# Selective-scan recurrences on one core: the skip term of block 0 moved between two rows of B, and the copy of a group's row of B moved behind the group's first decay

## The chip, the cores and the metric

The kernel runs on one core of a Trainium2 chip. The metric is device microseconds of one execution. The profile is one profiled execution of the same program.

## The reference

An image of 8 x 16 x 16 tokens with 64 channels passes a deformable convolution, a bidirectional Mamba layer and a graph-attention-gated mixture of four experts, each with a residual. The change is in the Mamba layer alone, whose core is, for each direction:

```
dt = softplus(dbc[..., :16] @ dt_proj_w.T + dt_proj_b)
Bm = dbc[..., 16:32];  Cm = dbc[..., 32:48];  A = -exp(A_log)
dA  = exp(dt[..., None] * A)                     # decay
dBu = dt[..., None] * Bm[:, :, None, :] * xs[..., None]
h_t = dA_t * h_{t-1} + dBu_t                     # along the 256 tokens of an image
y = einsum('blds,bls->bld', hs, Cm) + xs * D     # sum over the 16 states, and the skip term
y = y * silu(z)
```

There are 128 inner channels (the partitions), 16 states, 2 directions and 2048 tokens.

## The kernel before

The recurrences are cut into 4 blocks: direction 0 or 1 (`d`), first or second half of the batch (`hf`), so a tile of a block is 128 x 1024 fp32. A block takes its 16 states one after the other, in groups of four (`GROUP`). Five engines work on it in a pipeline, each with its own program; semaphores alone order them.

For state n of a block, with e = n mod 2 the buffer:

- TensorE spreads the state's row of B over all partitions into PSUM banks 6e and 6e+1 (`rows`, L775) and its row of C into banks 2 and 3 (`rows_c`, L783), each with 2 bf16 matmuls of 512 columns. Banks 4 and 5 collect y: the skip term opens them (L815, `diag_d` times `xs`, fp32), and `add_state` (L790) adds a state's C * h by an identity matmul, fp32.
- ScalarE computes the decay `da[e]` by Exp (L1050) and copies the row of C from PSUM to `cs[e]` (L1057), since GpSimd does not read PSUM here.
- VectorE multiplies B by dt * x in PSUM (L1425) and runs the scan into `hh[e]` (L1435).
- GpSimd multiplies `hh[e]` by `cs[e]` into `gg[e]` (L520), which `add_state` takes.

The last state of a group has another way for its row of B: TensorE puts the row into banks 2 and 3 (`rows_c` with slot 0 of the group), ScalarE copies it to `bx` (`b_copy`, L1043), GpSimd multiplies it by dt * x (`own_b`, L512) and ScalarE puts the product back into PSUM (L1054). Banks 2 and 3 so pass five rows a group in turn: the row of B, then four rows of C. `c_psum` counts the rows written and `c_ready` the rows copied out, and TensorE writes the next row only when the last one is copied out. The decays, the states and the gated products are double-buffered: the decay of state n waits for scan n-2 (`scan_ready`), the C copy of n and scan n for the C product of n-2 (`g_ready`), the C product of n for the add of n-2 (`g_used`).

TensorE's order at the start of a block (`first_rows`, then L808 on) is: row of B of state 3 (to be copied), row of B of state 0, row of C 0, row of B 1, row of C 1, row of B 2, row of C 2, row of C 3, the skip, adds 0 and 1. Between blocks `first_rows` of the next block stands ahead of the last two adds of the block. In the loop it is: row of B of the group's last state, then for each r of 4 the row of B (not for r = 3), the row of C, and the add of the state two before.

ScalarE's order is: `b_copy(0)` ahead of the first loop; `states(grp)`: for each r the decay, at r = 3 the put, and the C copy; then `b_copy` of the next group. Ahead of the loops of each direction ScalarE waits for dt of that direction and for `da_zero`, with which VectorE says that the first column of each image (no decay) is zero in both `da`; for direction 1 VectorE writes these zeros when all scans of block 1 are done (`no_decay`, L1417). Copies need no function table of their own; Exp and Silu (used just before the recurrences) have different ones.

`gated` (L1441) multiplies y by silu(z) when all adds of a block are done.

Of the kernel before, what the change touches and what calls it, by code (L numbers as in the profile page):

```python
# [14 lines left out]
DI, DS, DTR, TAPS = 128, 16, 16, 4  # L15
SEQP = SEQ + 2 * (TAPS - 1)
HALF = T // 2
# [28 lines left out]
GROUP = 4  # L46
# [30 lines left out]
def program(nc, a, out):  # L77
    with ExitStack() as ctx:
        def sb(name, shape, dt=F32):
            return ctx.enter_context(nc.sbuf_tensor(name, shape, dt))  # L80
# [5 lines left out]
        ps = ctx.enter_context(nc.psum_tensor("ps", [P, 8, 512], F32))  # L86

        def banks(lo, n, parts=P):
            return ps[0:parts, lo:lo + n, :].rearrange("p b n -> p (b n)")
# [43 lines left out]
        diag_d = [sb(f"diag_d{d}", [P, P]) for d in range(2)]  # L133
# [99 lines left out]
        xs, zs, dtv, uu = ([ar(T)] for _ in range(4))  # L233
# [339 lines left out]
        def _(pe):  # L573
# [183 lines left out]
            for c in range(CAP):  # L757
                m = pe.matmul(ps[:, 6, 0:2 * W], own1[:, c, :], pay[:, c, :, :].rearrange("p h w -> p (h w)"),
                              start=(c == 0), stop=(c == CAP - 1))
# [11 lines left out]
            def rows(d, hf, i0, n, e):  # L771

                pe.wait_ge(s["scan_ready"], n + 1)
                for q in range(2):
                    m = pe.matmul(ps[:, 6 * e + q, :], sel[:, i0].to_broadcast([96, P]),  # L775
                                  bc3[d][0:96, hf * HALF + 512 * q:hf * HALF + 512 * q + 512], start=True, stop=True)
                m.then_inc(s["b_psum"], 1)

            def rows_c(d, hf, i0, slot):

                pe.wait_ge(s["c_ready"], slot + 1)
                for q in range(2):
                    m = pe.matmul(ps[:, 2 + q, :], sel[:, i0].to_broadcast([96, P]),  # L783
                                  bc3[d][0:96, hf * HALF + 512 * q:hf * HALF + 512 * q + 512], start=True, stop=True)
                m.then_inc(s["c_psum"], 1)

            def add_state(n, e):
                pe.wait_ge(s["g_ready"], n + 3)
                for q in range(2):
                    m = pe.matmul(ps[:, 4 + q, :], ident[:], gg[e][:, 512 * q:512 * q + 512], start=False, stop=True, skip_group_check=True)  # L790
                m.then_inc(s["g_used"], 1)

            def first_rows(blk):
                d, hf = blk // 2, blk % 2
                pe.wait_ge(s["bc_ready"], d + 1)
                rows_c(d, hf, slice(GROUP - 1, GROUP), 4 * blk * SLOTS)
                for e in range(2):
                    rows(d, hf, slice(e, e + 1), 16 * blk + e, e)
                    rows_c(d, hf, slice(DS + e, DS + e + 1), 4 * blk * SLOTS + 1 + e)

            pe.wait_ge(s["z_ready"], 4)
            pe.wait_ge(s["rest_ready"], 4)
            pe.wait_ge(s["diag_ready"], 2)
            first_rows(0)
            for blk in range(4):
                d, hf = blk // 2, blk % 2

                rows(d, hf, slice(2, 3), 16 * blk + 2, 0)  # L808
                rows_c(d, hf, slice(DS + 2, DS + 3), 4 * blk * SLOTS + 3)
                rows_c(d, hf, slice(DS + 3, DS + 4), 4 * blk * SLOTS + 4)  # L810
                if blk:
                    pe.wait_ge(s["yg_ready"], blk)
                for q in range(2):
                    c0 = hf * HALF + 512 * q
                    pe.matmul(ps[:, 4 + q, :], diag_d[d][:], xs[d][:, c0:c0 + 512], start=True, stop=True)  # L815
                for e in range(2):
                    add_state(16 * blk + e, e)
                with pe.Fori(0, DS // GROUP - 1) as it:
                    n, slot = it * GROUP + 16 * blk, it * SLOTS + (4 * blk + 1) * SLOTS
                    rows_c(d, hf, bass.ds(it * GROUP + 7, 1), slot)  # L820
                    for r in range(GROUP):
                        if r < GROUP - 1:
                            rows(d, hf, bass.ds(it * GROUP + (4 + r), 1), n + (4 + r), r % 2)
                        rows_c(d, hf, bass.ds(it * GROUP + (DS + 4 + r), 1), slot + (1 + r))
                        add_state(n + (2 + r), r % 2)
                if blk < 3:
                    first_rows(blk + 1)
                    for e in range(2):
                        add_state(16 * blk + DS - 2 + e, e)
# [57 lines left out]
            for n in range(2 * EXP):  # L887
                h, e = n // EXP, n % EXP
# [12 lines left out]
        def _(act):  # L901
# [138 lines left out]
            def b_copy(grp):  # L1040

                act.wait_ge(s["c_psum"], grp * SLOTS + 1)
                f(bx, banks(2, 2), ACT.Copy).then_inc(s["c_ready"], 1)  # L1043

            def states(grp, src, lo, d, column):

                for r in range(GROUP):
                    n, e = grp * GROUP + r, r % 2
                    act.wait_ge(s["scan_ready"], n + 1)
                    f(da[e].rearrange("p (b s) -> p b s", s=SEQ)[:, :, lo:lo + SEQ - 1], src, ACT.Exp,  # L1050
                      scale=neg_a[d][:, column(r)]).then_inc(s["da_ready"], 1)
                    if r == GROUP - 1:
                        act.wait_ge(s["bx_ready"], grp + 1)
                        f(banks(6, 2), bx, ACT.Copy).then_inc(s["bx_put"], 1)  # L1054
                    act.wait_ge(s["c_psum"], grp * SLOTS + (r + 2))
                    act.wait_ge(s["g_ready"], n + 1)
                    f(cs[e], banks(2, 2), ACT.Copy).then_inc(s["c_ready"], 1)  # L1057

            act.wait_ge(s["nega_ready"], 4)
            for d in range(2):  # L1060
                act.wait_ge(s["dt_ready"], d + 1)
                act.wait_ge(s["da_zero"], 2 + d)
                lo = 1 - d
                for hf in range(2):
                    blk, c0 = 2 * d + hf, hf * HALF
                    src = dtv[d][:, c0:c0 + HALF].rearrange("p (b s) -> p b s", s=SEQ)[:, :, lo:lo + SEQ - 1]
                    if blk == 0:
                        b_copy(0)
                    with act.Fori(0, DS // GROUP if blk < 3 else DS // GROUP - 1) as it:
                        states(it + 4 * blk, src, lo, d, lambda r: bass.ds(it * GROUP + r, 1))  # L1070
                        b_copy(it + (4 * blk + 1))
                    if blk == 3:
                        states(15, src, lo, d, lambda r: slice(DS - GROUP + r, DS - GROUP + r + 1))
            f(pause[:, 3:4], ident[:, 0:1], ACT.Sqrt)
            act.wait_ge(s["ln_var"], 9)
            f(lns[:, 4, :], lns[:, 3, :], ACT.Sqrt).then_inc(s["ln_std"], 1)
# [651 lines left out]
```

## Time and profile before

| | |
|---|---|
| median of 3 runs | 688.21 us (681.62, 688.21, 688.95) |
| profiled execution, time | 686.99 us |
| its span, first to last instruction | 685.2 us |
| mean granted TensorE clock | 0.846 |
| busy: TensorE, VectorE, ScalarE, GpSimd | 528.6, 590.9, 320.2, 324.0 us |

The recurrences take about the stretch from 317 to 545 us of the span. A granted clock of 1.00 is 2.4 GHz and 0.50 is 1.2 GHz. Times in rows are microseconds from the start of the span. In a timeline a row is `start, duration, engine, line, operation, output<-inputs, shapes, count`, and in brackets the idle time of the engine before it with what ended it.

### The profile page before, as it was taken

How to read it: one execution, taken by the hardware profiler on the slowest of the kernel's cores; microseconds unless marked ns; L12 is line 12 of the kernel's file. 1: busy time of each engine (PE TensorE's matmuls, PEld its weight loads, DVE VectorE, ACT ScalarE, POOL GpSimd, SP SyncE). 2: the span in 40 equal slices, each digit the busy share in tenths (PEclk: the TensorE clock that was granted, in tenths of full speed). 3: DMA queues.
4: the chain of work that ended last, by engine and by line, in shares of the span. 5: the costliest groups of instructions: out<-in, count | busy, mean ns of one | idle time of the engine just before them, and what ended most of it. 6: DMA issues, size and time to landing. Idle time of an engine off the chain costs nothing.

```text
span 685.2 us, 11129 instructions
## 1 busy us (share of the span) xinstructions
PE 528.6 (77%) x4061; PEld 342.3 (50%) x4061; DVE 590.9 (86%) x1233; ACT 320.2 (47%) x380; POOL 324.0 (47%) x198
## 2 busy tenths in 40 slices
PE   2669999999999994987787788788888887973200
PEld 2148898898898992532323333233333474642200
DVE  4999799999799959998688989989989748379997
ACT  1431324333113125788577677777767603242210
POOL 5134042022020100235677789879978806777303
PEclk9855999999999996995799999999999985555555
DMA  7400000000000001000000000000000001111000
GB/s 210 101 14 1 2 3 2 3 10 2 2 10 2 2 9 44 0 0 1 0 0 0 0 1 0 0 0 0 1 0 0 0 1 16 9 9 8 4 0 31
DMA packets 17983, 8.56 MB, mean 12 GB/s; under 512 B 14832, under 2 KB 17168, under 8 KB 17680
## 3 DMA queue, kind: packets, MB, share of 16 engines
q1 hardware_dynamic: 16144, 7.35, 4.0%
q0 software_dynamic: 1792, 0.58, 1.5%
q8 instruction: 30, 0.49, 0.3%
q14 instruction: 17, 0.14, 0.1%
HBM read 6.67 MB, written 1.25 MB: 12 GB/s over the span
## 4 chain that ended last, share of the span: by engine, by line
PE 47%; DVE 27%; issue 10%; POOL 7%; ACT 6%; DMA 1%; ACTq 0%; POOLq 0%; DVEq 0%; SPq 0%
PE ps L637 10%; PE ps L629 9%; POOL arena L520 6%; PE ps L656 6%; PE ps L790 5%; DVE arena L1435 3%; PE ps L614 3%; DVE arena L1622 2%; DVE g L1624 2%; DVE ps L1425 2%; PE ps L880 2%; ACT arena L1050 2%; PE ps L893 1%; PE ps L783 1%; ACT arena L1057 1%
## 5 line engine op out<-in xcount | busy, mean ns | idle before, releaser
L520 POOL TENSOR_TENSOR arena<-arena 128x1024 f32<-128x1024 f32 x64 | 150.2, 2356 | 37.4 <-DVE arena L1435 13.4
L1435 DVE TENSOR_TENSOR_SCAN arena<-arena,ps 128x1024 f32<-128x1024 f32 x64 | 144.6, 2280 | 16.0 <-ACT arena L1050 11.8
L790 PE MATMUL ps<-arena,ident 128*128 128x512 f32 x256 | 122.0, 603 | 16.0 <-POOL arena L520 15.6
L485 POOL TENSOR_TENSOR arena<-arena 128x1280 f32<-128x1280 f32 x16 | 39.7, 2505 | 155.9 <-DVE arena L1285 140.1
L790 PEld LDWEIGHTS ps<-arena,ident 128*128 128x128 f32 x256 | 46.8, 191 | 68.2 <-issue 36.3
L954 ACT ACTIVATE arena<-ps 128x768 f32<-128x768 f32 x48 | 37.7, 809 | 89.5 <-PE ps L656 89.5
L1057 ACT ACTIVATE arena<-ps 128x1024 f32<-128x1024 f32 x64 | 65.1, 1018 | 29.1 <-POOL arena L520 23.5
L558 POOL DMA_INDIRECT arena<-node_rows,src_idx x56 | 56.0, 1000 | 37.1 <-DMA node_rows<-hrow 20.3
L1050 ACT ACTIVATE arena<-arena,neg_a 128x1020 f32<-128x1020 f32 x64 | 72.9, 1139 | 0.6 <-DVE arena L1417 0.4
L783 PE MATMUL ps<-arena,sel 96*128 96x512 bf16 x160 | 50.1, 395 | 26.0 <-ACT arena L1057 12.5
L629 PE MATMUL ps<-arena 128*128 128x64 f32 x576 | 70.0, 283 | 0.0
L637 PE MATMUL ps<-arena 128*32 128x64 bf16 x2048 | 69.8, 319 | 0.0
L629 PEld LDWEIGHTS ps<-arena 128*128 128x128 f32 x576 | 69.3, 201 | 0.1
L637 PEld LDWEIGHTS ps<-arena 128*32 128x32 bf16 x2048 | 67.7, 145 | 3.1 <-issue 3.1
L1270 DVE TENSOR_SCALAR arena<-lo_b 128x296 bf16<-128x296 bf16 (+1 forms) x448 | 65.8, 228 | 0.0
L1425 DVE TENSOR_TENSOR ps<-arena,ps 128x1024 f32<-128x1024 f32 x48 | 58.1, 1210 | 7.3 <-PE ps L775 7.3
L656 PE MATMUL ps<-ident,arena 128*128 128x128 f32 x288 | 46.2, 315 | 5.4 <-POOL arena L485 4.7
L656 PEld LDWEIGHTS ps<-ident,arena 128*128 128x128 f32 x288 | 37.5, 161 | 17.9 <-issue 11.3
L783 PEld LDWEIGHTS ps<-arena,sel 96*128 (+1 forms) x160 | 13.4, 99 | 63.8 <-issue 33.7
L1268 DVE TENSOR_SCALAR arena<-hi_b 128x296 bf16<-128x296 bf16 (+1 forms) x224 | 35.4, 237 | 10.6 <-PE ps L637 10.6
L937 ACT ACTIVATE arena<-ps 128x288 f32<-128x288 f32 x32 | 13.1, 410 | 55.4 <-PE ps L629 27.6
L880 PEld LDWEIGHTS ps<-w,arena 128*128 128x128 f32 x128 | 28.2, 331 | 19.5 <-ACT arena L1086 11.5
(333 smaller groups left out, 809.7 us busy)
## 6 DMA issues: line engine op xcount, KB each, us to landing
arena<-dram_edges SPq DMA_DIRECT2D x2, 1024.0 KB, 8.6
arena<-dram_x SPq DMA_DIRECT2D x2, 512.0 KB, 4.8
arena<-node_rows,src_idx POOLq DMA_INDIRECT x56, 2.7
x_tok<-dram_x SPq DMA_DIRECT2D x1, 512.0 KB, 10.9
res_scratch<-x_tok SPq DMA_DIRECT2D x4, 128.0 KB, 2.0
arena<-res_scratch SPq DMA_DIRECT2D x1, 512.0 KB, 3.3
w<-dram_w SPq DMA_DIRECT2D x3, 128.0 KB, 2.7
arena<-dram_f_conv_w SPq DMA_DIRECT2D x1, 256.0 KB, 11.0
```

The source lines that it names most:

```text
L520: g.tensor_tensor(gg[r % 2], hh[r % 2], cs[r % 2], ALU.mult).then_inc(s["g_ready"], 1)
L558: g.indirect_dma_start(out=nb[:, w, :], out_offset=None, in_=tab_d, in_offset=bass.IndirectOffsetOnAxis(ap=src_idx[:, w:w + 1], axis=0)).t ...
L629: m = pe.matmul(o, s_t[i % 2][:, 2 * t + tau, :], xk[b % 2][:, tau, C * t:C * t + C], start=(t == 0 and tau == 0), stop=(t == K2 - 1 and t ...
L637: m = pe.matmul(ps[32 * q:32 * q + 32, 4, 0:LO], one_hi[:, :, e + q], one_lo[:, :, e + q], start=(ch == 0 and e == 0), stop=(ch == len(CHU ...
L656: m = pe.transpose(ps[:, 2 * (n % 2) + v // 4, (v % 4) * P:(v % 4) * P + P], s_rows[i % 2][:, t // 2, (t % 2) * P:(t % 2) * P + P], ident[:])
L783: m = pe.matmul(ps[:, 2 + q, :], sel[:, i0].to_broadcast([96, P]), bc3[d][0:96, hf * HALF + 512 * q:hf * HALF + 512 * q + 512], start=True ...
L790: m = pe.matmul(ps[:, 4 + q, :], ident[:], gg[e][:, 512 * q:512 * q + 512], start=False, stop=True, skip_group_check=True)
L1050: f(da[e].rearrange("p (b s) -> p b s", s=SEQ)[:, :, lo:lo + SEQ - 1], src, ACT.Exp, scale=neg_a[d][:, column(r)]).then_inc(s["da_ready"], 1)
L1057: f(cs[e], banks(2, 2), ACT.Copy).then_inc(s["c_ready"], 1)
L1270: m = ts(one_lo[:, x - HI, 0:en], lo_b[:, e0:e0 + en], float(x - HI), None, ALU.is_equal)
L1425: tt(b, uu[d][:, c0:c0 + HALF], b, ALU.mult).then_inc(s["b_made"], 1)
L1435: v.tensor_tensor_scan(o, x0, x1, 0.0, ALU.mult, ALU.add).then_inc(s["scan_ready"], 1)
```

## The change

Three edits: the skip term becomes a function; for block 0 it is issued in `first_rows` between row of B 0 and row of C 0, for the other blocks it stays where it was. `b_copy` of a group moves into `states`, behind the group's first decay and ahead of its first C copy. With that the B copy ahead of the first loop and those at the end of the loops go, and block 3's last group needs no code of its own. The number of copies, decays and matmuls is the same.

```diff
+            def skip_path(blk):
+                d, c0 = blk // 2, (blk % 2) * HALF
+                for q in range(2):
+                    pe.matmul(ps[:, 4 + q, :], diag_d[d][:], xs[d][:, c0 + 512 * q:c0 + 512 * q + 512], start=True, stop=True)
+
             def first_rows(blk):
                 d, hf = blk // 2, blk % 2
                 pe.wait_ge(s["bc_ready"], d + 1)
                 rows_c(d, hf, slice(GROUP - 1, GROUP), 4 * blk * SLOTS)
                 for e in range(2):
                     rows(d, hf, slice(e, e + 1), 16 * blk + e, e)
+                    if e == 0 and blk == 0:
+                        skip_path(0)
                     rows_c(d, hf, slice(DS + e, DS + e + 1), 4 * blk * SLOTS + 1 + e)
@@ L810
                 rows_c(d, hf, slice(DS + 3, DS + 4), 4 * blk * SLOTS + 4)
                 if blk:
                     pe.wait_ge(s["yg_ready"], blk)
-                for q in range(2):
-                    c0 = hf * HALF + 512 * q
-                    pe.matmul(ps[:, 4 + q, :], diag_d[d][:], xs[d][:, c0:c0 + 512], start=True, stop=True)
+                    skip_path(blk)
                 for e in range(2):
                     add_state(16 * blk + e, e)
@@ L1049, states
                     f(da[e].rearrange("p (b s) -> p b s", s=SEQ)[:, :, lo:lo + SEQ - 1], src, ACT.Exp,
                       scale=neg_a[d][:, column(r)]).then_inc(s["da_ready"], 1)
+                    if r == 0:
+                        b_copy(grp)
                     if r == GROUP - 1:
@@ L1064
-                    if blk == 0:
-                        b_copy(0)
-                    with act.Fori(0, DS // GROUP if blk < 3 else DS // GROUP - 1) as it:
+                    with act.Fori(0, DS // GROUP) as it:
                         states(it + 4 * blk, src, lo, d, lambda r: bass.ds(it * GROUP + r, 1))
-                        b_copy(it + (4 * blk + 1))
-                    if blk == 3:
-                        states(15, src, lo, d, lambda r: slice(DS - GROUP + r, DS - GROUP + r + 1))
```

## Rows read from the trace of the kernel before

**Rows 1.** the page, busy time of each engine, its share of the span and its instructions

```profile
PE 528.6 (77%) x4061; PEld 342.3 (50%) x4061; DVE 590.9 (86%) x1233; ACT 320.2 (47%) x380; POOL 324.0 (47%) x198
```

**Rows 2.** list of waits: engine, line, waited for; us in total, times, longest

```profile
DVE arena L1435 <- ACT arena L1050: 11.8, 16, 2.2
```

**Rows 3.** timeline of TensorE, start of block 0

```profile
317.87 1.06 PE L775 MATMUL ps<-arena,sel 96*128 96x512 bf16 x2
319.96 1.04 PE L783 MATMUL ps<-arena,sel 96*128 96x512 bf16 x2 [1.04 <-ACT arena L1043]
...
329.00 1.03 PE L783 MATMUL ps<-arena,sel 96*128 96x512 bf16 x2 [2.37 <-ACT arena L1057]
329.82 3.62 PE L815 MATMUL ps<-arena,diag_d 128*128 128x512 f32 x4
333.24 3.80 PE L790 MATMUL ps<-arena,ident 128*128 128x512 f32 x8
```

**Rows 4.** windows: PE, PEld, DVE, ACT, POOL busy (instructions), PEclk, DMA

```profile
310.00:313.00 3.00, 3.00 (x4) 1.08 (x4) 2.96 (x2) 2.97 (x3) 0.38 (x1) 0.50 0.00 0
333.50:334.00 0.50, 0.50 (x2) 0.21 (x2) 0.44 (x1) 0.00 (x0) 0.00 (x0) 0.87 0.00 0
```

**Rows 5.** timelines of GpSimd and VectorE, block 0 and first scan of block 1

```profile
335.47 4.65 POOL L520 TENSOR_TENSOR arena<-arena 128x1024 f32<-128x1024 f32 x2 [4.65 <-PE ps L790]
...
337.94 1.23 DVE L1425 TENSOR_TENSOR ps<-arena,ps 128x1024 f32<-128x1024 f32 x1 [4.00 <-PE ps L775]
341.02 2.29 DVE L1435 TENSOR_TENSOR_SCAN arena<-arena,ps 128x1024 f32<-128x1024 f32 x1 [1.86 <-ACT arena L1050]
...
355.46 2.29 DVE L1435 TENSOR_TENSOR_SCAN arena<-arena,ps 128x1024 f32<-128x1024 f32 x1 [1.77 <-ACT arena L1050]
...
382.76 2.29 DVE L1435 TENSOR_TENSOR_SCAN arena<-arena,ps 128x1024 f32<-128x1024 f32 x1 [0.19 <-ACT arena L1050]
```

**Rows 6.** timelines of ScalarE and TensorE, block 0, start of group 2

```profile
351.95 1.02 ACT L1043 ACTIVATE arena<-ps 128x1024 f32<-128x1024 f32 x1 [1.39 <-PE ps L783]
352.99 1.28 ACT L1050 ACT_TABLE_LOAD   x1
354.28 1.15 ACT L1050 ACTIVATE arena<-arena,neg_a 128x1020 f32<-128x1020 f32 x1
...
353.11 0.60 PE L783 MATMUL ps<-arena,sel 96*128 96x512 bf16 x2 [0.77 <-ACT arena L1043]
...
355.27 0.60 PE L775 MATMUL ps<-arena,sel 96*128 96x512 bf16 x2
```

**Rows 7.** timelines of VectorE, GpSimd and ScalarE, block 0, second state of group 2

```profile
357.67 1.21 DVE L1425 TENSOR_TENSOR ps<-arena,ps 128x1024 f32<-128x1024 f32 x1
359.01 2.29 DVE L1435 TENSOR_TENSOR_SCAN arena<-arena,ps 128x1024 f32<-128x1024 f32 x1
...
361.53 2.35 POOL L520 TENSOR_TENSOR arena<-arena 128x1024 f32<-128x1024 f32 x1 [1.17 <-ACT arena L1057]
...
363.97 1.02 ACT L1057 ACTIVATE arena<-ps 128x1024 f32<-128x1024 f32 x1 [0.49 <-POOL arena L520]
```

**Rows 8.** timelines of ScalarE and VectorE, block 1, starts of groups

```profile
409.07 1.02 ACT L1043 ACTIVATE arena<-ps 128x1024 f32<-128x1024 f32 x1 [1.39 <-PE ps L783]
...
398.14 2.29 DVE L1435 TENSOR_TENSOR_SCAN arena<-arena,ps 128x1024 f32<-128x1024 f32 x1 [0.43 <-ACT arena L1050]
...
411.16 2.29 DVE L1435 TENSOR_TENSOR_SCAN arena<-arena,ps 128x1024 f32<-128x1024 f32 x1 [0.35 <-ACT arena L1050]
```

**Rows 9.** timelines of ScalarE, TensorE and GpSimd, passage to block 2

```profile
434.95 1.02 ACT L1043 ACTIVATE arena<-ps 128x1024 f32<-128x1024 f32 x1 [0.89 <-PE ps L783]
436.41 1.15 ACT L1050 ACTIVATE arena<-arena,neg_a 128x1020 f32<-128x1020 f32 x1 [0.44 <-DVE arena L1417]
...
438.52 0.60 PE L783 MATMUL ps<-arena,sel 96*128 96x512 bf16 x2 [1.46 <-ACT arena L1057]
...
440.93 2.35 POOL L520 TENSOR_TENSOR arena<-arena 128x1024 f32<-128x1024 f32 x1 [0.31 <-PE ps L790]
```

## The prediction

> **What bounds the kernel now.** The busy times come first: VectorE 86% and TensorE 77% of the span, ScalarE and GpSimd 47% each [rows 1]. That is an average over stages; the change touches only the recurrences (about 317 to 545 us), so the rest was read there. The list of waits says what VectorE lacks in that stretch: before its 64 scans it sat idle 11.8 us, always until ScalarE's decay (L1050) [rows 2]. Then the timelines of the engines, side by side, give the order of one group of four states. Names used below: *B copy* (L1043), *decay* (L1050), *put* (L1054), *C copy* (L1057) on ScalarE; *row* of B or C (L775, L783), *skip* (L815), *add* (L790, one state, four matmuls) on TensorE; *product* (L1425) and *scan* (L1435) on VectorE; the products with B (L512) and C (L520) on GpSimd.
>
> VectorE alone needs, for a group, 4 scans and 3 products: a scan takes 2.20 us until the next instruction starts (355.46 to 357.67), a product 1.34 until its scan starts [rows 5, 7], so 4 x 2.20 + 3 x 1.34 = 12.8 us. GpSimd needs 5 x 2.35 = 11.8 [rows 7]. Block 0 runs at 355.46 - 341.02 = 14.44 us a group [rows 5]. The excess is a wait of 1.77 before the group's first scan [rows 5], and rows 6 show its cause: the last C copy of the group ends 1.39 before 351.95, ScalarE idles those 1.39 for the row of B, does the B copy (1.02), loads a function table (1.28) and only then the decay (1.15), which ends as the scan starts. In block 1 no table is loaded and the same wait is 0.35 [rows 8]. Apart from that, the first block has one long hole: TensorE does the skip (3.4) and two adds (3.8) from 329.8 to 337.0 [rows 3], at a granted clock of 0.50 that rises to 1.00 just after 333.5 (0.87 is the mean of that half microsecond) [rows 4]; GpSimd idles 4.65 for the first add, VectorE 4.00 for the next row of B and then 1.86 for the decay [rows 5].
>
> **Part 1: the skip term of block 0, from behind the rows to between them.** The same four matmuls (3.41 us at the low clock: 333.24 - 329.82 [rows 3]) now follow the two rows of B, the second of which starts at 317.87 and takes 0.85 or so: 318.8 [rows 3]. TensorE's next instruction, the first row of C, waits for the B copy. That copy, which ends just before 319.96 today, comes behind the table load and the first decay, 1.3 + 1.05 later: near 322.3. The skip ends at 318.8 + 3.4 = 322.2: hidden. Without that cover (B copy early) it would cost up to 322.2 - 319.96 = 2.2 us to the first row of C. What is late next: nothing before 329.0. The last row of C, with 2.37 idle before it [rows 3], waits for a C copy behind GpSimd's first products, and GpSimd starts those behind work that does not move. So the adds start at 329.82 and not at 333.24. Their time depends on the clock. If it rises at 333.57 as now, the first add ends at 333.2 (low clock, 3.4), the second at 335.1; row of B and row for the product by 336.1; product; scan at 337.5. The decay is ready long before: ScalarE has nothing else to do from the group's last C copy on, and load and decay take 2.4. That is 3.5 us before 341.02 [rows 5]. Bounds: with the high clock throughout, the adds end at 333.3, and the second scan of the group, which then waits for the row behind the B copy, gains 4.9; with the low clock throughout, the adds end at 336.7, the scan starts near 339.2 and gains 1.8. I take 3.5, since the pattern of work from 329.0 on is as dense as before.
>
> **Part 2: the decay ahead of the B copy, block 0.** The decay and its table load leave the path (B row, B copy, load, decay, scan). From the end of the last C copy, load and decay take 2.4 us and fit before the product is done, so group 2's scan is set by VectorE: 12.8 after 337.5, at 350.3; 14.44 - 12.8 = **1.6** gained. But the B copy now stands behind load and decay, and behind it the row of C, an add, the row for the second product, all in TensorE's order. From the end of the last C copy: load 1.30, decay to the next start 1.05 (1.15 less the 0.1 by which a copy and a decay back to back overlap), B copy 1.02, gap to the row of C 0.14, row of C and add 355.27 - 353.11 = 2.16, row for the product 0.6 [rows 6] = 6.3; product to scan 1.34, scan to GpSimd's product 361.53 - 359.01 = 2.52, that to the C copy 363.97 - 361.53 = 2.44, C copy 1.02 [rows 7] = 7.3. The loop takes 13.65 us: a new bound, 0.8 above VectorE's 12.85. So group 3 (counted from 0) gains 14.44 - 13.65 = **0.8**, and the passage to block 1, where VectorE's idle is only 0.19 today (no table is loaded) [rows 5], loses **0.8**. Block 0 in all: 3.5 + 1.6 + 0.8 - 0.8 = **5.1 us** gained at the first scan of block 1.
>
> The rows give the load 1.29 from its start to the decay's, with no gap before it [rows 6]; the sum uses that. The Trainium skill ("ScalarE: Activation LUTs", What ACT_TABLE_LOAD costs) gives 1283 ns for the load and another 1380 ns of drain for a switch; by that price three loads on the new loop would cost 4.1 more, and the whole change would gain 1.3, which is rival (d). The trace has the 1.28 and not the drain.
>
> **Part 3: the same in blocks 1 to 3.** The decay takes 1.05 of ScalarE's 1.39 of idleness before the B copy [rows 8], so the B copy stays where it is and GpSimd and TensorE see nothing. VectorE's idle before the scan is 0.43 at a block's second group and 0.35 at the next two [rows 8], of which 1.34 - 1.21 = 0.13 stays, as between any product and its scan [rows 7]: 0.3 + 0.2 + 0.2 = **0.7** a block, 2.1 in three. Bounds: 0, if ScalarE's decay is held up by the loop's turn, and 0.43 + 0.35 + 0.35 = 1.1 a block.
>
> **Part 4: the passage from block 1 to block 2.** Here the moved copy meets a wait. The decay of the backward direction waits for the zeros that VectorE writes (L1417) behind the last scan of block 1; ScalarE waits for that before it enters the loop. Today the B copy is done before (434.95 to 435.97), now it is queued behind the wait and the decay: decay 436.41, B copy 437.46 to 438.5 [rows 9]. Behind it on TensorE stand a row of C, a row of B, the next row of C (438.52 today, behind the first C copy; now B copy 438.5, gap and row 0.74, C copy 1.02, gap 0.06: 440.3), and two adds. GpSimd idles 0.31 for the first add already [rows 9], so the chain from there to the skip and the adds of block 2 has no slack. Cost 440.3 - 438.52 = **1.8 us**. Bounds: 0, were the chain to have slack that I do not see, and 2.5, the whole shift of the B copy.
>
> **Sum.** -5.1 - 2.1 + 1.8 = **-5.4 us**. The profiled run took 686.99 (span 685.2, 1.8 around it), so the new kernel would take 681.6; the median of three runs is 688.21, 1.2 higher, which gives 682.8. I say **682**. The tail behind 545 us depends on the recurrences' end alone and moves as a whole.
>
> **Rivals.** *(a) The clock rises earlier.* With the skip between the rows TensorE works almost without a gap from 317 to 326, where today it idles 1.04 and more [rows 3]. If the clock rises then and holds, part 1 gives 4.9 and not 3.5; and a run of before in which it rises late (up to 3.4 later, a low-clock add) loses 1.7 more to it: -6.8 to -8.5, 679 to 681. Against it: from 310 to 313 TensorE was busy throughout and the clock stayed at 0.50 [rows 4], and behind the rows comes an idle of over 2 us [rows 3]. The Trainium skill ("TensorE: Matmul & The Clock Gate", Part 1) says the throttled state is the default and activity releases it, which speaks for this rival; the trace agrees as far as its one rise in this stretch, behind the skip, goes.
> *(b) The loads leave block 0's loop* or are hidden otherwise: then block 0 runs at 12.8, and the loss of 0.8 at its end goes as does 0.8 in group 3: -7, 680. Against it: the loop body is entered with the table of Silu, and the load stands at the first Exp of the body today [rows 6].
> *(c) Slower: the B copy slips in every group.* Its cover is ScalarE's idle of 1.39 against a decay of 1.05 [rows 8]. If the decay can't start when the C copy ends, the B copy slips by up to 1.05; it decides once the cover left is under 1.05. Of the row for the second product only 0.4 is slack: it ends at 409.07 + 1.02 + 0.14 + 2.16 + 0.6 = 413.0, and VectorE takes it at 411.16 + 2.20 = 413.4 [rows 6 to 8]. Eleven groups of blocks 1 to 3 at 0.65 are +7.2 in the place of -2.1: -5.1 + 7.2 + 1.8 = +3.9, 692. For it speaks only the thin margin of 0.34.
> *(d) The load costs more in its new place than its row shows*: a second 1.3 in three groups of block 0, +3.9, leaves -1.5: 686. Against it: the row.
>
> **How the numbers follow.** Forecast 0.54, (a) 0.22, (b) 0.06, (c) 0.06, (d) 0.12. The range takes in (a), (b) and half of (d): 677.5 to 686.5; runs of this kernel spread over 681.6 to 689.0, so about 1% (6.9 us) is what can be told from no change. The forecast of -5.4 lies inside; with its own spread of 2 us a quarter of it lies beyond: 0.13 + 0.18 of (a) + 0.03 of (b) gives 0.34 faster, 0.62 same, 0.04 slower.
>
> **What would show it.** Skip matmuls at about 318.8, none between rows and adds; GpSimd's idle of 4.65 down to about 2.5 and VectorE's 4.00 to about 2.2; first scans of block 0's groups 1 to 3 near 337.5, 350.3, 364.0, block 1's near 377.6; product to scan 1.34 everywhere; table loads still four, each ahead of the B copy; in block 2 the B copy at decay + 1.05 and the skip 1.8 later than today against the scan that opens the block. Wrong would be: a different clock history between 317 and 337, a B copy late in the plain groups, or no loss at block 2.

## The result, and the profile after

| | before | after |
|---|---|---|
| median of 21 runs each, alternating | 683.13 us (679.07 to 689.35) | 677.21 us (671.19 to 685.84) |
| mean of the same runs | 684.1 | 678.9 |
| profiled execution, span | 685.2 us | 674.5 us |
| mean granted TensorE clock of it | 0.846 | 0.865 |

The ratio is 0.988, 95% interval 0.985 to 0.991. It leaves out 9 runs of after as disturbed, so it shows more than the means do: they differ by 5.1 us, 0.75%, with a standard error of 1.25. Both kernels' 21 runs lie in two heaps: before has 11 at 679.1 to 683.1 and 10 at 685.5 to 689.4, after 11 at 671.2 to 677.2 and 10 at 680.5 to 685.8, and each median is the uppermost run of its lower heap. With all later runs of after (30) its heaps hold 14 and 16, with nothing between, and the mean is 679.4 +- 0.9; some 90 runs of before, later ones among them that fill its gap, have a mean of 683.8 +- 0.3. The better figure for the change is this 4.4 us.

The profiles differ by 10.7 us, and that is no measure of the change. I cut each span at four landmarks on VectorE: the last write of zeros ahead of the recurrences (L1417 before, L1420 after; where the head ends), the first scan of blocks 1, 2 and 3, and the start of the last two scans (where the tail begins). Beside the two profiles stand four more of each kernel, from the experiments:

| us | span | head | block 0 | block 1 | block 2 | block 3 | blocks, sum | tail |
|---|---|---|---|---|---|---|---|---|
| before | 685.2 | 318.65 | 64.11 | 54.83 | 54.20 | 48.50 | 221.6 | 144.9 |
| before, e7 | 677.3 | 309.34 | 63.89 | 54.81 | 55.89 | 48.50 | 223.1 | 144.9 |
| before, e11 | 684.8 | 317.94 | 64.41 | 54.82 | 54.20 | 48.52 | 222.0 | 144.9 |
| before, e13 | 677.5 | 309.48 | 63.87 | 54.81 | 55.90 | 48.52 | 223.1 | 144.9 |
| before, e15 | 679.5 | 312.89 | 64.19 | 54.83 | 54.18 | 48.51 | 221.7 | 144.9 |
| after | 674.5 | 313.07 | 60.83 | 54.18 | 56.73 | 47.86 | 219.6 | 141.8 |
| after, e6 | 669.9 | 309.65 | 58.84 | 54.16 | 57.63 | 47.86 | 218.5 | 141.8 |
| after, e12 | 673.3 | 313.12 | 60.84 | 54.15 | 56.74 | 47.85 | 219.6 | 140.6 |
| after, e14 | 683.7 | 318.40 | 58.99 | 54.16 | 57.71 | 49.42 | 220.3 | 145.0 |
| after, e16 | 680.2 | 314.77 | 59.01 | 54.15 | 57.74 | 49.43 | 220.3 | 145.1 |

Of the 10.7 us, 5.6 lie in the head, where not one instruction is changed, 2.0 in the recurrences and 3.1 in the tail. The means of five and five say: head 313.7 and 313.8, so nothing; recurrences 222.3 and 219.7, **-2.6**; tail 144.9 and 142.9, **-2.0**. That is -4.5, near the -4.4 of the times. The agreement is no test: the heads scatter by 3 to 4 us from profile to profile, so that two means of five could have differed by 2 or 3 us by chance. The recurrences scatter by 0.7 only, and their -2.6 is clear of that.

The head first. A window of before, then the same of after (columns: us, busy time with instructions of PE, PEld, DVE, ACT, POOL, granted clock, DMA share, GB/s), and below each the same 36 matmuls from the timeline of TensorE:

```profile
45.00:62.00 17.00, 17.00 (x67) 13.98 (x66) 17.00 (x98) 5.28 (x8) 1.74 (x2) 0.50 0.00 0
...
54.42 7.78 PE L629 MATMUL ps<-arena 128*128 128x64 f32 x36
```

```profile
45.00:62.00 17.00, 12.42 (x152) 10.41 (x155) 17.00 (x98) 5.15 (x9) 1.73 (x2) 0.80 0.01 2
...
49.82 4.13 PE L629 MATMUL ps<-arena 128*128 128x64 f32 x36
```

The same 36 matmuls took 7.78 us at a granted clock of 0.50 and 4.13 in after, where the clock had risen. (The counts 67 and 152 exaggerate the difference: some 80 of the 152 are short matmuls of the next line, which after had already reached.) The slow head is no mark of before: e14, a profile of after, has one of 318.40. Whoever compares two profiles of this kernel has to take that out first.

**The recurrences of after.** The page's busy times (to [rows 1]) and the list of waits (to [rows 2]):

```profile
PE 508.2 (75%) x4061; PEld 326.8 (48%) x4061; DVE 591.1 (88%) x1233; ACT 321.3 (48%) x380; POOL 323.8 (48%) x198
...
L1438 DVE TENSOR_TENSOR_SCAN arena<-arena,ps 128x1024 f32<-128x1024 f32 x64 | 144.7, 2281 | 8.2 <-ACT arena L1056 2.4
```

```profile
DVE ps L1428 <- PE ps L775: 10.1, 6, 3.0
...
DVE arena L1438 <- ACT arena L1056: 2.4, 4, 1.5
```

The wait that the change aims at is down from 11.8 us in 16 places to 2.4 in 4. VectorE's wait for a row of B from TensorE has grown, from 7.3 us in 5 places to 10.1 in 6. Before had:

```profile
DVE ps L1425 <- PE ps L775: 7.3, 5, 4.0
```

Where those of after come from, the timeline of TensorE shows (to [rows 3]):

```profile
312.15 1.06 PE L775 MATMUL ps<-arena,sel 96*128 96x512 bf16 x2
313.00 2.66 PE L797 MATMUL ps<-arena,diag_d 128*128 128x512 f32 x4
316.88 0.61 PE L783 MATMUL ps<-arena,sel 96*128 96x512 bf16 x2 [1.22 <-ACT arena L1049]
...
323.43 1.04 PE L783 MATMUL ps<-arena,sel 96*128 96x512 bf16 x2 [2.27 <-ACT arena L1065]
324.26 5.56 PE L790 MATMUL ps<-arena,ident 128*128 128x512 f32 x8
...
345.14 0.93 PE L783 MATMUL ps<-arena,sel 96*128 96x512 bf16 x2 [1.72 <-ACT arena L1049]
345.86 3.29 PE L790 MATMUL ps<-arena,ident 128*128 128x512 f32 x4
```

The skip (L797) stands between the rows and is hidden: TensorE still waits 1.22 behind it. The clock rose during it (2.66 for what takes 3.62 at the low clock; the rows behind it take 0.60), and was low again at 323.43, behind the idle of 2.27, where a row that takes 0.60 takes 1.04. So the two adds took 5.56 and not the 3.80 of [rows 3]. GpSimd and VectorE (to [rows 5]):

```profile
328.03 4.66 POOL L520 TENSOR_TENSOR arena<-arena 128x1024 f32<-128x1024 f32 x2 [3.45 <-PE ps L790]
...
330.73 1.23 DVE L1428 TENSOR_TENSOR ps<-arena,ps 128x1024 f32<-128x1024 f32 x1 [2.98 <-PE ps L775]
332.09 2.29 DVE L1438 TENSOR_TENSOR_SCAN arena<-arena,ps 128x1024 f32<-128x1024 f32 x1
...
344.89 2.29 DVE L1438 TENSOR_TENSOR_SCAN arena<-arena,ps 128x1024 f32<-128x1024 f32 x1
349.62 1.23 DVE L1428 TENSOR_TENSOR ps<-arena,ps 128x1024 f32<-128x1024 f32 x1 [2.44 <-PE ps L775]
...
360.25 2.29 DVE L1438 TENSOR_TENSOR_SCAN arena<-arena,ps 128x1024 f32<-128x1024 f32 x1
...
373.90 2.29 DVE L1438 TENSOR_TENSOR_SCAN arena<-arena,ps 128x1024 f32<-128x1024 f32 x1
```

The idle times of 4.65 and 4.00 are now 3.45 and 2.98, and the 1.86 before the scan is gone. Group 1 to group 2 takes 12.80. Then comes 15.36, since the add at 345.86 fell to the low clock too (3.29; 1.88 is usual). The last group takes 13.65. The adds of block 0 start 11.19 behind the last zeros (324.26 - 313.07), as forecast (329.82 - 318.65 = 11.17). ScalarE at the start of group 1, and in the passage to block 2 (to [rows 6, 9]):

```profile
326.29 1.28 ACT L1056 ACT_TABLE_LOAD   x1
327.58 1.15 ACT L1056 ACTIVATE arena<-arena,neg_a 128x1020 f32<-128x1020 f32 x1
330.30 1.02 ACT L1049 ACTIVATE arena<-ps 128x1024 f32<-128x1024 f32 x1 [1.57 <-PE ps L783]
...
426.90 1.15 ACT L1056 ACTIVATE arena<-arena,neg_a 128x1020 f32<-128x1020 f32 x1 [2.13 <-DVE arena L1420]
427.96 1.00 ACT L1049 ACTIVATE arena<-ps 128x1024 f32<-128x1024 f32 x1
```

The load keeps its 1.28 and the decay follows 1.29 behind its start. At 427.96 the B copy stands behind the wait for zeros and the decay, as forecast. What that does to TensorE:

```profile
425.41 0.59 PE L775 MATMUL ps<-arena,sel 96*128 96x512 bf16 x2
429.01 0.61 PE L783 MATMUL ps<-arena,sel 96*128 96x512 bf16 x2 [3.01 <-ACT arena L1049]
...
430.74 1.04 PE L783 MATMUL ps<-arena,sel 96*128 96x512 bf16 x2 [0.69 <-ACT arena L1065]
431.57 4.82 PE L790 MATMUL ps<-arena,ident 128*128 128x512 f32 x8
```

It idles 3.01, and behind that idle the clock falls: the adds take 4.82 where 3.60 is usual.

**The tail.** The same code of the experts' matmuls in before, then in after:

```profile
578.46 3.52 PE L880 MATMUL ps<-w,arena 128*128 128x64 f32 x16
581.90 2.08 PE L893 MATMUL ps<-arena,w 64*128 64x512 f32 x4
```

```profile
570.79 1.90 PE L886 MATMUL ps<-w,arena 128*128 128x64 f32 x16
572.62 1.13 PE L899 MATMUL ps<-arena,w 64*128 64x512 f32 x4
```

In after the clock rose there, in before it stayed at 0.50, and these and the next matmuls of the experts took near twice as long; the tail as a whole differs by 3.1 us.

### The profile page after: what moved, and what is told of

Its sections match the earlier page's. It is cut to its first block, busy times and chain, and to the rows that moved or that the text cites. A ratio compares the mean times of both kernels' runs of the same rounds, so it can differ in the third digit from the quotient of the medians.

```text
span 674.5 us, 11144 instructions
## 1 busy us (share of the span) xinstructions
PE 508.2 (75%) x4061; PEld 326.8 (48%) x4061; DVE 591.1 (88%) x1233; ACT 321.3 (48%) x380; POOL 323.8 (48%) x198
## 3 DMA queue, kind: packets, MB, share of 16 engines
HBM read 6.67 MB, written 1.25 MB: 12 GB/s over the span
## 4 chain that ended last, share of the span: by engine, by line
PE 40%; DVE 26%; POOL 13%; issue 13%; ACT 5%; DMA 2%; DVEq 0%; POOLq 0%; ACTq 0%; SPq 0%
PE ps L637 10%; PE ps L629 8%; POOL arena L558 8%; PE ps L790 5%; PE ps L656 5%; POOL arena L520 5%; DVE arena L1438 4%; DVE ps L1428 4%; PE ps L614 2%; PE ps L711 1%; DVE arena L1273 1%; PE ps L783 1%; ACT arena L1065 1%; PE ps L861 1%; DVE arena L1271 1%
## 5 line engine op out<-in xcount | busy, mean ns | idle before, releaser
L520 POOL TENSOR_TENSOR arena<-arena 128x1024 f32<-128x1024 f32 x64 | 150.1, 2361 | 35.3 <-PE ps L790 16.3
L790 PE MATMUL ps<-arena,ident 128*128 128x512 f32 x256 | 126.3, 621 | 11.8 <-POOL arena L520 11.7
L790 PEld LDWEIGHTS ps<-arena,ident 128*128 128x128 f32 x256 | 48.6, 197 | 65.5 <-issue 38.8
L1428 DVE TENSOR_TENSOR ps<-arena,ps 128x1024 f32<-128x1024 f32 x48 | 58.1, 1211 | 10.2 <-PE ps L775 10.1
L629 PE MATMUL ps<-arena 128*128 128x64 f32 x576 | 66.3, 274 | 0.0
L629 PEld LDWEIGHTS ps<-arena 128*128 128x128 f32 x576 | 65.6, 192 | 0.1
L656 PE MATMUL ps<-ident,arena 128*128 128x128 f32 x288 | 42.2, 297 | 5.4 <-POOL arena L485 4.7
L656 PEld LDWEIGHTS ps<-ident,arena 128*128 128x128 f32 x288 | 34.3, 151 | 17.1 <-issue 11.7
L512 POOL TENSOR_TENSOR arena<-arena 128x1024 f32<-128x1024 f32 x16 | 37.9, 2366 | 0.4 <-ACT arena L1049 0.2
```

Of the source, the lines that this page charges most:

```text
L520: g.tensor_tensor(gg[r % 2], hh[r % 2], cs[r % 2], ALU.mult).then_inc(s["g_ready"], 1)
L629: m = pe.matmul(o, s_t[i % 2][:, 2 * t + tau, :], xk[b % 2][:, tau, C * t:C * t + C], start=(t == 0 and tau == 0), stop=(t == K2 - 1 and t ...
L656: m = pe.transpose(ps[:, 2 * (n % 2) + v // 4, (v % 4) * P:(v % 4) * P + P], s_rows[i % 2][:, t // 2, (t % 2) * P:(t % 2) * P + P], ident[:])
L1428: tt(b, uu[d][:, c0:c0 + HALF], b, ALU.mult).then_inc(s["b_made"], 1)
```

## The experiments

**The two parts alone.** e1: before with the skip between the rows, ScalarE's order as it was. e2: before with the B copy behind the first decay of every group, the skip where it was.

```
e1   first_rows, e == 0 and blk == 0:      + skip_path(0)       (ScalarE as before)
e2   states, behind the decay of r == 0:   + b_copy(grp)        (TensorE as before)
     L1067 to L1073                        - b_copy(0), - b_copy(it + (4 * blk + 1)),
                                           - the last group of block 3 written out
```

> The kernel before with the skip term of block 0 moved and nothing of ScalarE's order changed. In the profiles so far the stretch from VectorE's last zero (L1417 before, L1420 after) to the first scan of block 1 is 64.1 us before and 60.8 us after, block 1 54.8 and 54.2, block 2 54.2 and 56.7, block 3 to its last pair of scans 48.5 and 47.9. Theory A (the skip's move is worth about 3.5 us in block 0 when the clock has the same history, and parts 2 to 4 are as predicted): here TensorE has no cover for the skip at the start (row of C up to 2.2 us later) but GpSimd's first products set the adds anyway, so the stretch to block 1 is 60.5 to 62, blocks 1 to 3 are as before (54.8, 54.2, 48.5). Theory B (the gain of block 0 comes from the decay's new place and the skip's move is eaten by the lower clock that finds the adds): the stretch stays at 63.5 to 64.5. Time: A about 3 us below the kernel before, B within 1 us.

> The kernel before with the B copy behind the group's first decay and the skip term where it was. Theory A: the stretch to the first scan of block 1 is 62 to 63 (the first decay's table load out of the path at group 1 and 2, the new loop of 13.65 us in the last two), block 1 54.2, block 2 54.2 + 1.8 - 0.7 = 55.3 at a steady clock or 56.7 if the longer idle before it lets the clock fall, block 3 47.9. Theory B (all gain of block 0 from the decay): stretch 60.5 to 61. Rival: the loss of block 2 comes with the skip's move and not with the copy's: block 2 54.2 here.

First scans of groups 1, 2, 3 and of block 1, from the last zeros:

| us | group 1 | group 2 | group 3 | block 1 |
|---|---|---|---|---|
| before | 22.37 | 36.81 | 51.26 | 64.11 |
| e1, skip alone | 20.60 | 35.04 | 49.49 | 62.34 |
| e2, copy alone | 20.58 | 33.38 | 47.04 | 60.70 |
| e6, both (after again) | 18.71 | 31.52 | 45.18 | 58.84 |
| gain: e1, e2, e6 | 1.8, 1.8, 3.7 | 1.8, 3.4, 5.3 | 1.8, 4.2, 6.1 | 1.8, 3.4, 5.3 |

The gains add up. Neither theory of e1 gave its 62.34 (60.5 to 62, or 63.5 to 64.5): the skip alone is worth half of what theory A gave it. e2's 60.70 lies where theory B had it, but not for B's reason, since the skip gains too; theory A had put too little (62 to 63) on the copy. The 1.8 of the skip are 3.4 of skip less the 1.6 by which the adds are slower (5.43 against 3.80). The other 1.8 at group 1, which I had put into part 1, is the copy's: load and decay have left VectorE's path there too. In e2 the adds still lie behind the skip, and are fast; ScalarE did the decay long before:

```profile
328.42 3.62 PE L815 MATMUL ps<-arena,diag_d 128*128 128x512 f32 x4
331.83 3.72 PE L790 MATMUL ps<-arena,ident 128*128 128x512 f32 x8
```

```profile
330.45 1.28 ACT L1050 ACT_TABLE_LOAD   x1
331.74 1.15 ACT L1050 ACTIVATE arena<-arena,neg_a 128x1020 f32<-128x1020 f32 x1
336.03 1.02 ACT L1043 ACTIVATE arena<-ps 128x1024 f32<-128x1024 f32 x1 [3.14 <-PE ps L783]
```

Times: e1 685.05 median of 12, ratio 0.999 (0.996 to 1.002), where 3 us below before had been expected; e2 682.22 of 12, 0.995 (0.991 to 0.998). The ratios here and below are to runs of before taken beside each experiment; the means stand in a table below. e2 pays block 2's passage: 56.66, 2.5 over before.

**The queue at block 2.** e3 is after with the B copy of group 8 ahead of the wait for zeros.

```
   act.wait_ge(s["dt_ready"], d + 1)
+  if d:
+      b_copy(8)
   act.wait_ge(s["da_zero"], 2 + d)
```

The group that follows is written out without a B copy, and the loop runs over groups 9 to 11.

> The changed kernel, but the B copy of the first group of block 2 stands ahead of ScalarE's wait for the zeros of the backward direction, as in the kernel before. If the loss of block 2 (56.7 against 54.2) is that copy queued behind the wait and the decay, block 2 falls to 53.5 (54.2 less 0.7), 3.2 below the changed kernel, of which 1.8 is the queue and the rest the clock that fell in the 3.0 us that TensorE idled there. If the loss was only this run's clock, it stays above 55.5. Time: about 2 to 3 us below the changed kernel.

TensorE of e3 in the passage:

```profile
425.53 0.60 PE L783 MATMUL ps<-arena,sel 96*128 96x512 bf16 x2 [0.74 <-ACT arena L1049]
425.97 0.59 PE L775 MATMUL ps<-arena,sel 96*128 96x512 bf16 x2
427.49 1.04 PE L783 MATMUL ps<-arena,sel 96*128 96x512 bf16 x2 [0.92 <-ACT arena L1065]
428.32 4.85 PE L790 MATMUL ps<-arena,ident 128*128 128x512 f32 x8
```

The idle of 3.01 is 0.74, and block 2 takes 54.98 in the place of 56.73 to 57.74. The adds were slow here too, behind an idle of 0.92, so the queue is not the only thing that lets the clock fall at this place; before had slow adds here in two of five profiles (5.29, which is its 55.89). But it makes the fall more frequent: all eight profiles of kernels with the copy queued there (five of after, e2, e4, e5) have slow adds in this passage, against two of seven with the order of before (e1 and e10 among them) and one of three with the mended order (e3, e8, e9). Where they are not slow (e8, e9, with the same order) block 2 takes 53.35. So the queue costs 56.73 - 54.98 = 1.75 with slow adds in both. The 53.5 expected came out in e8 and e9, not in e3. Time: 676.11 median of 6, ratio 0.985 (0.980 to 0.990).

**The loads out of the loop.** e4 is after with one small exponential ahead of the recurrences, which brings the table in once. e10 is the same line in before.

```
+  f(pause[:, 3:4], ident[:, 0:1], ACT.Exp)
   act.wait_ge(s["nega_ready"], 4)
```

> The changed kernel with one Exp of a single column ahead of ScalarE's loops, so that the function table is loaded once and the loop of block 0 has no load in it. Theory A (the load, decay and B copy in a row set the pace of block 0): groups of block 0 go at VectorE's 12.8 us, no table load in the loop, the stretch from the last zero to block 1 is 58 to 59.5 against 60.8. Rival: GpSimd or the clock sets the pace of block 0, and the stretch stays within 0.5 of 60.8. Time: 1 to 3 us below the changed kernel.

> The kernel before with one table load ahead of ScalarE's loops and nothing else. In the order of before each load of block 0 stands on the path to the scan: its groups fall from 14.44 to 13.1 or so (VectorE's 12.8 plus the idle of 0.35 of the later blocks), and the first boundary by 1.3: block 0 64.0 - 1.0 (first scan) - 3 x 1.3 = 59 to 60.3, other blocks as before. If that is so, the table load alone is worth as much in block 0 as the copy's new place (60.7 with the copy moved alone). Time: 3 to 5 us below the kernel before.

ScalarE of e4, end of group 1, no load ahead of the decay, and VectorE's first scans of groups 1 and 2:

```profile
338.52 1.02 ACT L1065 ACTIVATE arena<-ps 128x1024 f32<-128x1024 f32 x1
339.50 1.15 ACT L1056 ACTIVATE arena<-arena,neg_a 128x1020 f32<-128x1020 f32 x1
```

```profile
330.00 2.29 DVE L1439 TENSOR_TENSOR_SCAN arena<-arena,ps 128x1024 f32<-128x1024 f32 x1
...
342.81 2.29 DVE L1439 TENSOR_TENSOR_SCAN arena<-arena,ps 128x1024 f32<-128x1024 f32 x1
```

Every group of block 0 takes 12.80 to 12.81, VectorE's own sum; block 0 ends at 57.14, 1.7 before e6. The loads are what keeps block 0 at 13.66. But this profile of e4 shows no gain over all four blocks: two slow adds (5.30 for 3.60) fell in at the passage to block 1, which takes 55.79 for 54.16, and block 2 takes 57.69, so that the recurrences take 218.5, as in e6. In e10 block 0 takes 59.84: one line gains 4.3 there, more than the copy's move alone (3.4), and leaves the passage to block 2 as it was (54.20). Times: e4 675.16 median of 12, 0.986 (0.982 to 0.990); e10 681.06 of 12, 0.994 (0.990 to 0.998); by the medians alone e10 gains nothing on the 681.21 of before beside it, by the means 3.7 us.

**The idle ahead of the adds filled.** e5 is after with the skip issued a second time, in block 0, just before the last row of C; it writes the same values to the same place, so the output is the same.

```
   rows_c(d, hf, slice(DS + 2, DS + 3), 4 * blk * SLOTS + 3)
+  if blk == 0:
+      skip_path(0)
   rows_c(d, hf, slice(DS + 3, DS + 4), 4 * blk * SLOTS + 4)
```

> The changed kernel with the skip term of block 0 computed a second time, ahead of the block's last row of C, where TensorE idled 2.3 us in the changed kernel; it overwrites the first with the same values, so nothing else changes. It is a filler: 1.7 us of matmuls at the high clock, 3.4 at the low one. Clock theory (the skip raises the clock early, it falls again in the idle that follows, and the eight adds pass at the low clock: 5.3 to 5.6 us against 3.8 before): with the filler the adds take 3.4 to 3.8 us and the first scan of group 1 comes at 17 to 17.7 after the last zero against 19.0 (18.8 without the other things that differ). Rival (the clock's history there is chance or set by what lies before): the adds stay at 5.3 or so, and the filler costs up to 1 us, 19 to 20.

```profile
318.32 3.15 PE L797 MATMUL ps<-arena,diag_d 128*128 128x512 f32 x4
321.31 0.60 PE L783 MATMUL ps<-arena,sel 96*128 96x512 bf16 x2
321.74 3.60 PE L790 MATMUL ps<-arena,ident 128*128 128x512 f32 x8
```

TensorE works without a gap from the filler on, and the adds take 3.60. The filler did not keep the clock up, though. The row of C ahead of it took 1.03, so the clock was low before the filler began (in e6 too: 1.03 ahead of the idle of 1.55), and it rose near the filler's end (3.15; 1.88 would be the high clock, 3.62 the low one). So the filler does what the skip did in before, whose 3.62 at the low clock stood ahead of adds of 3.80: it takes the low clock upon itself. This run can't tell whether the idle or the missing work made the adds slow. The filler also delays them, and group 1 gains 0.8 against e6 (17.88 for 18.71). A slow add then fell in at group 2 (3.37), and block 0 took 59.70. Time: 678.78 median of 12, 0.990 (0.986 to 0.994); its mean of 677.5 against 680.1 of e6 beside it is within the noise, so no gain over after is shown.

**All three, and the two that paid.** e8 is e3 + e4 + e5, e9 is e3 + e4.

> The changed kernel with all three: one table load ahead of the loops, the B copy of block 2's first group ahead of the wait for the zeros, and the second skip term as a filler. Without slow adds: block 0 at 16.5 for the first scan of group 1 and 12.8 a group, 55.5 to 56; blocks 53.9, 53.5 to 55, 47.9; 211 to 213 for the four, against 219.6 of the changed kernel and 221.6 before. Time 7 us below the changed kernel. If the clock falls at the passages between blocks as in the kernel with one table load (5.3 us for eight adds), 214 to 216.

> The changed kernel with one table load ahead of ScalarE's loops and the B copy of block 2's first group ahead of the wait for the zeros, without the filler. From the single runs: block 0 57.1, block 1 53.9, block 2 53.4 without slow adds, block 3 47.9: 212.3 for the four stretches if no adds are slow at the passages, up to 1.8 more for each passage at which they are. Rival: the two mends share one gain (the shorter block 0 only moves the slow adds to later passages, as one table load alone did: 218.5): then 215 or more. Time: 5 to 7 us below the changed kernel at a like head and tail.

VectorE of e9, first scans of groups 1 to 3 and of block 1:

```profile
337.65 2.29 DVE L1446 TENSOR_TENSOR_SCAN arena<-arena,ps 128x1024 f32<-128x1024 f32 x1
...
350.45 2.29 DVE L1446 TENSOR_TENSOR_SCAN arena<-arena,ps 128x1024 f32<-128x1024 f32 x1
...
363.26 2.29 DVE L1446 TENSOR_TENSOR_SCAN arena<-arena,ps 128x1024 f32<-128x1024 f32 x1
...
376.06 2.29 DVE L1446 TENSOR_TENSOR_SCAN arena<-arena,ps 128x1024 f32<-128x1024 f32 x1
```

12.80 a group throughout. e9's recurrences take 212.5 us, e8's 212.9 (block 0 in 56.2, but slow adds of 5.29 at block 3). In e9 the two adds of block 0 are slow (5.55, behind an idle of 3.54); at all later passages they take 3.60. Times: e8 678.25 median of 6, 0.990 (0.984 to 0.995); e9 **672.23** of 6, 668.5 to 674.5, 0.986 (0.983 to 0.990), the fastest kernel here by its median, 5 below after. The 7 us below after that were expected of e8 did not come: 678.25 lies 1 above it.

Means against the runs of before taken beside each (us, with the standard error of the difference):

| e1 | e2 | e3 | e4 | e5 | e6 | e8 | e9 | e10 | e7, before itself |
|---|---|---|---|---|---|---|---|---|---|
| -0.7 +- 0.9 | -2.6 +- 1.1 | -8.8 +- 1.9 | -8.3 +- 1.3 | -6.8 +- 1.5 | -4.2 +- 2.7 | -7.5 +- 1.5 | -10.3 +- 1.2 | -3.7 +- 1.2 | -1.8 +- 1.3 |

**More profiles of the two kernels, unchanged.** e6, e12, e14 and e16 are after; e7, e11, e13 and e15 are before.

> The changed kernel once more, for a second profile and more times. If the stretches follow the program and not chance, the recurrences from the last zero to the last pair of scans take 219 to 220 as in the first profile, with slow adds at the same places (block 0's first, passage to block 2, which took 5.6 and 4.8); if the one slow add in group 2 (3.3 us against 1.9) was chance, block 0 is 59 and not 60.8. The stretches ahead of the recurrences and behind them may differ by up to 6 and 3 us from the first profile, since only the clock's history differs there.

> The kernel before once more, for a second profile. If the first is typical, block 0 takes 64.1, the blocks 54.8, 54.2, 48.5, with no slow adds behind the first. The head (to the last zero, 318.7 in the first profile) lies at 312 to 319: if it comes out below 315, the first profile of before was one of the long heads and its 5.6 us against the changed kernel's head are no effect of the change.

> The kernel before, for a third profile: blocks 63.9 to 64.1, 54.8, 54.2 or 55.9 (with slow adds at the passage to block 2), 48.5. Head between 309 and 319. If the tail is a matter of the program's length, it is 144.9 again as in the two profiles so far; if it is chance, it may come out near 141.7 as in the changed kernel's.

> The changed kernel, for a third profile: block 0 58.9 or 60.8 (with a slow add in group 2), block 1 54.2, block 2 56.7 to 57.6, block 3 47.9; head between 309 and 319; tail 141.8 again if it follows the program, up to 144.9 if it is chance.

> The kernel before once more, unchanged. Theory 1, the shorter tail belongs to the change: the stretch from the last pair of scans to the end is 144.9 us again in this and the two other looks at before, and 140.6 to 141.8 in the three looks at after. Theory 2, chance of the clock: at least one of the six shows the other kernel's tail. Head: 309 to 319, either way by chance.

> The changed kernel once more. Theory 1: tail 140.6 to 141.8, the granted clock rises in the experts' matmuls. Theory 2: in one of the three looks at after the tail is near 145. Block 0 to the first scan of block 1: 58.8 where the adds follow at 5.3, 60.8 where a third slow add falls in, in both theories.

> As for the fourth look at before: tail 144.9 by theory 1; 140.6 to 141.8 in at least one look by theory 2.

> As for the fourth look at after: tail 140.6 to 141.8 by theory 1; near 145 in at least one look by theory 2.

Times: e6 682.53 median of 6, e7 681.32 of 8, the others one run each: e11 686.55, e12 675.01, e13 679.27, e14 685.49, e15 681.25, e16 681.93. Their stretches stand in the table above. By the third profile of each kernel the tail seemed to be the change's (144.9 against 140.6 to 141.8), the theory that e13 to e16 call the first. It fell: e14 and e16 have tails of 145.0 and 145.1. TensorE of e14:

```profile
490.29 1.03 PE L783 MATMUL ps<-arena,sel 96*128 96x512 bf16 x2 [0.69 <-ACT arena L1065]
491.11 4.86 PE L790 MATMUL ps<-arena,ident 128*128 128x512 f32 x8
...
577.02 3.52 PE L886 MATMUL ps<-w,arena 128*128 128x64 f32 x16
```

Both profiles have slow adds at block 3 as well (49.4 for 47.9), as e8 has, whose tail is 145.1 too. Block 3 and tail together make after come in two kinds 4.8 to 6.1 us apart. That is a part of the distance between the heaps, not all of it: the three profiled runs in the lower heap and the two in the upper one are 9.4 us apart in the mean, 5.2 of it by block 3 and tail, and 4.6 by the head. e2 has the long tail without slow adds at block 3, so the one does not simply cause the other. All profiles of kernels without the moved copy (five of before, e1, e10) have the long tail; of the eleven with it (five of after, e2 to e5, e8, e9) seven have the short one, 140.6 to 141.8. Were the tail's kind independent of the copy's place, so clean a split would come about once in a hundred times. So the change probably opens the short tail without making it certain; by what way is not shown, and before might still show it in a longer series.

## Why the prediction was right and wrong

The forecast of -5.4 us was near what the times show: 4.4 to 5.1 by the means, 5.9 by the medians. The time of 682 was not: 677.21 lies 0.3 below the range. The step that failed is **Sum**, at "the median of three runs is 688.21, 1.2 higher, which gives 682.8". The base was 683 to 684 (683.13 by the median of 21 runs, 683.8 by the mean of all), not 688: with these the same change gives 677.7 to 678.4, inside the range. I took one profile and three runs for the kernel's time, while its head alone varies by 9.3 us from profile to profile (309.3 to 318.7), and my profile had the longest head of the five. That the tail "moves as a whole" was the second part of that failure: with the clock it varied between 140.6 and 145.1.

Term by term, against profiles in which nothing else fell in:

| term | forecast | measured |
|---|---|---|
| group 1 of block 0 (part 1) | -3.5 | -3.7 (e6); skip 1.8, copy 1.8 |
| group 2 | -5.1 | -5.3 |
| block 1 (end of part 2) | -5.1 | -5.3; -3.3 where a third add was slow |
| loop of block 0 with the load | 13.65 | 13.66 (e6), 12.80 without load (e4) |
| part 3, a block | -0.7 | -0.65 |
| part 4, queue at block 2 | +1.8 | +1.75 (after against e3) |
| part 4, low clock behind the idle | 0 | +1.2 to +1.8 |
| block 3's passage | 0 | +1.6 in two profiles of five |

**Part 1** was right in its size, and the two adds took what I had summed (5.26 in e6, 5.3 by my sum: low clock for the first, high for the second). The way there was another, which I had named as a sign of being wrong: the clock rose already during the skip and fell again before the adds. That the adds then met the same split is luck. VectorE's idle ahead of group 1 came out at 2.98 (2.49 in e6) and not at 2.2. And part 1 was wrong in what it was made of; half of the gain belongs to the copy. **Part 2** and **part 3** held to 0.2 us; the terms of part 2's loop, 6.3 and 7.3, add up to 13.6, a little under the 13.65 that I wrote and the 13.66 that came. **Part 4** held for the queue and left out what the idle does to the clock. I had asked that question at the start of block 0 and not here. Over five profiles, block 0 gained 4.4 (forecast 5.1, two slow adds in group 2), block 2 lost 2.4 (forecast 1.1), and block 3's gain of 0.65 was eaten up on average: that is how -5.4 became -2.6 in the recurrences. The tail then gave 2.0 back, which no step of mine had. So the total of -5.4 came near the measured one partly by luck.

**Rivals.** (a) The rise came, in the skip of after and e1, but did not hold up to the adds, and they were slow. In after it was lost over the idle of 2.27 that I had set against it; in e6 already one row earlier, behind an idle of 0.91. The Trainium skill ("TensorE: Matmul & The Clock Gate", Part 1) has activity release the throttle. The rise during the skip, and in e5 during the filler (3.15), agree with that. (b) The loads stayed in the loop; e4 shows that taking them out gives what I had put on it. (c) The B copy did not slip in the plain groups: block 1 gained 0.65. (d) No drain: the decay starts 1.29 behind the load's start. The Trainium skill ("ScalarE: Activation LUTs", What ACT_TABLE_LOAD costs) has another 1380 ns there for a switch to a different set. The loop time of 13.66 leaves no room for it. The three loads in the loop's later passes bring in a table that is in already, so the page need not mean them; but the first load of before is such a switch, and it starts 0.02 behind the copy ahead of it, with the decay 1.30 behind its start (319.92 to 321.22).

## What to carry to other kernels

Before a time is forecast, cut the profile at landmarks around the change and ask how much the unchanged stretches vary between executions; here that was 9 us in the head and 4.5 in the tail, around a change of 2.6 in between. When an edit lengthens an idle of TensorE ahead of dense matmuls, price the matmuls behind it at both clocks: here the wait itself cost 1.75 and the fall of the clock as much again. And when a loop on ScalarE is entered with another function table, look for a load in every pass: one small exponential ahead of the loop was worth 4.3 us in the first block in the one profile of e10, more than the move of the copy.

## What was not expected of the hardware

The same instructions at the same place run at either clock level from one execution to the next: in the passage to block 2 of before the two adds took 5.29 in two profiles and kept to their usual 3.60 in three, behind idles of 1.44 to 1.46 in all five. In after, slow adds followed idles of 2.3, 1.7 and 0.7 us (431.57 stands behind 0.69, and an idle of 3.01 lies just ahead of that), while other idles of 1.1 to 1.7 had none behind them: of the two idles of 1.72 at the same place in groups 2 and 3 the first has a slow add behind it (345.86) and the second (360.49) has not. The length of the last idle alone does not tell. Each such fall cost 1.2 to 1.8 us.
